# A two-layer graph network on one NeuronCore: edge keys before the normalisation, the adjacency zeroed by GpSimd, its totals made by DMA, relations fetched two ahead

## The reference

```python
def rgcn(x):                                  # in block 1
    out = x @ root + bias
    for r in range(8):
        mask = (edge_type == r)
        sums = segment_sum(x[src] * mask, dst)
        cnt = segment_sum(mask, dst)
        out = out + sums / max(cnt, 1) @ weight[r]
    return out
# block 1: a gated relational GNN
xn = layernorm(x); u = rgcn(xn)
z = concat([u, xn]) @ w_gate + b_gate
x = x + tanh(u) * z + xn * (1 - z)
# block 2: x = x + int8_linear(layernorm(x)), one scale for the whole input, from its largest magnitude
# block 3: x = x + D^-1/2 A D^-1/2 (layernorm(x) @ W.T + b), A the edges of all relations with self loops
# block 4: x = x + top-2 mixture of 8 experts + 0.1 * a shared expert, of layernorm(x)
```

## Time and profile before

| | us |
|---|---|
| median of 3 runs | 1464.07 (1456.95 to 1470.3) |
| the profiled execution | 1455.25 |
| its span | 1453.2 |
| PE busy, instructions | 1152.1 (79%), 5203 |
| DVE, POOL, ACT busy | 765.1, 432.5, 388.9 |
| mean granted TensorE clock | 0.888 |
| DMA | 200.76 MB, mean 138 GB/s |

### The profile page before, as it was taken

One profiled execution on the slowest core, in us unless ns is written; L12 is line 12 of the kernel. 1 busy time (PEld: TensorE's weight loads), 2 busy tenths in 40 slices (PEclk: granted clock), 3 DMA queues, 4 the chain that ended last, 5 costly groups with the idle time before them and its releaser, 6 DMA issues.

```text
span 1453.2 us, 13715 instructions
## 1 busy us (share of the span) xinstructions
PE 1152.1 (79%) x5203; PEld 906.0 (62%) x5203; DVE 765.1 (53%) x1230; ACT 388.9 (27%) x647; POOL 432.5 (30%) x284
## 2 busy tenths in 40 slices
PE   2659999999999999629466677756982899778993
PEld 1447777777777777517345455544861687657872
DVE  2429767867776412112345445443628747646644
ACT  1112232232223223011222222211414333315751
POOL 1005554445464555600111111110054501230023
PEclk8779999999999999859678888867995999979996
DMA  8554476765554444222322222234360210177855
GB/s 313 207 190 132 129 188 190 220 173 174 162 127 144 139 97 134 22 97 96 119 98 103 105 102 100 112 134 146 100 187 0 72 58 30 41 202 253 291 177 159
DMA packets 82465, 200.76 MB, mean 138 GB/s; under 512 B 33658, under 2 KB 34271, under 8 KB 73694
## 3 DMA queue, kind: packets, MB, share of 16 engines
q1 hardware_dynamic: 27444, 131.49, 26.1%
q0 software_dynamic: 35040, 21.99, 9.5%
q10 hardware_dynamic: 19908, 46.30, 9.0%
HBM read 141.21 MB, written 58.52 MB: 137 GB/s over the span
## 4 chain that ended last, share of the span: by engine, by line
PE 36%; DMA 31%; DVE 14%; POOL 8%; issue 5%; ACT 2%; ACTq 2%; SPq 1%; POOLq 0%; DVEq 0%
PE ps L481 30%; DMA stage<-h_scratch 8%; DMA adj_scratch<-cnt,idx 5%; POOL adj_scratch L1754 5%; DVE rl L334 5%; DMA AT<-adj_scratch 4%; DMA acb<-adj_scratch 3%; DMA stage<-in_w_e 3%; DMA stage<-in_w_gate 2%; DMA X<-in_x 2%; ACTq L948 1%; DVE U L1301 1%; DMA xn_scratch<-U 1%; ACT rh L326 1%; PE ps L743 1%
## 5 line engine op out<-in xcount | busy, mean ns | idle before, releaser
L334 DVE TENSOR_TENSOR rl<-stage,rh 128x512 fp32r<-128x512 f32 (+1 forms) x330 | 255.6, 805 | 488.4 <-ACT rh L326 488.3
L481 PE MATMUL ps<-rh,xTh 128*125 128x512 f32 x880 | 353.9, 402 | 75.3 <-DVE He L1273 39.6
L326 ACT CAST rh<-stage 128x512 fp32r<-128x512 f32 (+1 forms) x344 | 203.1, 622 | 646.6 <-PE ps L481 241.8
L481 PE MATMUL ps<-rl,xTh 128*125 128x512 f32 x880 | 351.7, 400 | 0.0
L481 PE MATMUL ps<-rh,xTl 128*125 128x512 f32 x880 | 349.8, 398 | 0.0
L1754 POOL DMA_INDIRECT adj_scratch<-cnt,idx x164 | 266.9, 1628 | 276.7 <-DMA adj_scratch<-cnt,idx 122.9
L481 PE MATMUL ps<-rh,Ar 125*125 125x512 f32 x400 | 173.9, 435 | 110.7 <-DVE rc L1291 96.0
L481 PEld LDWEIGHTS ps<-rh,xTh 128*125 128x125 f32 x880 | 165.9, 188 | 119.9 <-DVE He L1273 40.0
L481 PEld LDWEIGHTS ps<-rh,xTl 128*125 128x125 f32 x880 | 165.8, 188 | 43.0
L481 PEld LDWEIGHTS ps<-rl,xTh 128*125 128x125 f32 x880 | 165.8, 188 | 40.5
L481 PE MATMUL ps<-rl,Ar 125*125 125x512 f32 x400 | 170.0, 425 | 2.3 <-issue 2.3
(11 more groups left out here) (265 smaller groups left out, 1260.2 us busy)
## 6 DMA issues: line engine op xcount, KB each, us to landing
stage<-in_w_rel SPq DMA_DIRECT2D x32, 1024.0 KB
h_scratch<-He ACTq DMA_DIRECT2D x80, 250.0 KB
stage<-in_w_e SPq DMA_DIRECT2D x16, 1024.0 KB
adj_scratch<-Z ACTq DMA_DIRECT2D x16, 763.5 KB, 13.3
stage<-h_scratch SPq DMA_DIRECT2D x16, 750.0 KB
KR<-key_scratch ACTq DMA_DIRECT2D x41, 256.0 KB, 5.3
stage<-in_w_gate SPq DMA_DIRECT2D x8, 1024.0 KB
stage<-h_scratch SPq DMA_DIRECT2D x16, 500.0 KB
```

Of the source, the lines that this page charges most:

```text
L326: e.copy(h, s).then_inc(*a_hi.up(("hi", i)))
L334: e.tensor_tensor(l, s, h.bitcast(F32), ALU.subtract).then_inc(*own.up(("lo", i)))
L481: ins = e.matmul(ps[0:P, b, :], a, m, start=first and n == 0, stop=last and n == len(parts) - 1)
```

## The change

The edge keys come first: ACT issues the edge loads, DVE makes the keys before it normalises the first chunk, and PE turns them before anything else. The windows have TG = 5 tiles, so that there are 33 of them in place of 41, two to a half of a unit, and the first is made ahead of the second half of unit 0; the keys fill 83 rows in place of 82. The sixteen zeroing DMAs are issued by POOL once all of x is in. The normalised input is no longer stored: `x` is loaded again during relation 1, and ACT makes `XL` (the normalised input) and `X` (x plus it) from that and the statistics kept in `keep`. He has 6 slots. In stage 2 SP loads adjacency 0 and 1 after the first half of h(0), and then relation r + 2 after h(r). The counts come from `Sr`, the sum of the five chunks of `Ar` that DVE makes (`sources_summed`), times a column of ones. The total is made by eight DMAs of POOL from `adj_scratch`, the last seven accumulating. `Atot` lies where `AT` is to be, and is turned in place, five blocks at a time, after each chunk of block 2; DVE's degree sum and inverse roots move into and behind the gate. DVE adds into U before it makes the low parts, not after.

The sizes:

```diff
-TILES = 164
-TG = 4
+TILES = 165
+TG = 5
+KROWS = 83
-NHE = 8
+NHE = 6
-WINDOWS = (0, 2, 5)
+WINDOWS = (0, 4)
```

SP:

```diff
             def adjacency_in(r):
                 on.wait_ge(*at("added", TILES - 1))
+                on.wait_ge(*at("slot zero"))
                 if r >= 2:
                     on.wait_ge(*at("adj", r - 2))
...
-            adjacency_in(0)
             for r in range(R):
                 for g in range(first("h", r, 0, 0), first("h", r, 0, 0) + 4):
+                    if r == 0 and g == first("h", 0, 1, 0):
+                        adjacency_in(0)
+                        adjacency_in(1)
                     if g < first("gate", 0, 0) - 1:
                         load(g)
-                if r + 1 < R:
-                    adjacency_in(r + 1)
+                if r + 2 < R:
+                    adjacency_in(r + 2)
+                if r == 1:
+                    on.wait_ge(*at("unit", R + 1, 1, C - 1))
+                    e.dma_start(XL[:], x_v).then_inc(*d_xl.up(("x again",)))
...
-            on.wait_ge(*at("xn"))
-            e.dma_start(XL[:].rearrange("p c d -> p (c d)"), xnd).then_inc(*d_xl.up(("xl",)))
...
-            for c in range(C):
-                on.wait_ge(*at("spread", R - 1, 1, C - 1))
-                e.dma_start(X[:, c, :], x_v[:, c, :]).then_inc(*d_xc[c].up(("x again", c)))
```

PE, the counts of stage 2 (in place of ten column sums and five turns a relation), and the turns of the total behind each chunk of block 2:

```diff
+            def counts(r):
+
+                b, freed = banks.take(("counts", r), ("numbers", r))
+                on.wait_ge(*at("sources summed", r))
...
+                for c in range(C):
+                    ins = e.matmul(ps[0:P, b, 2 * c:2 * c + 2], Sr[:, r % 2, c * P:(c + 1) * P], ones2[:], start=True, stop=True)
...
+            for r in range(R):
+                if r:
+                    counts(r)
                 freed = lambda hf: lambda c: ("u", r + 1, c, hf)
+                by_tile(("spread", r, 0), tile["h", r, 0, 0], C, a_stat(r), freed(0), (("adj", r),), most_turned if r == R - 1 else None)
+                if r == 0:
+                    counts(0)
                 if r < R - 1:
                     by_tile(("spread", r, 1), tile["h", r, 1, 0], C, a_stat(r), freed(1), (("adj", r),))
...
+                for n, (i, j) in enumerate(swaps(c)):
+                    ins = e.transpose(ps[0:P, pair[n // 4][0], n % 4 * P:n % 4 * P + P], part_of(Atot, i, j), ident[0:P, 0:P])
```

ACT (of each `def` and loop the lines that matter):

```diff
+            for i, a in enumerate((src, dst, typ)):
+                on.wait_ge(*at("er zero", i))
+                e.dma_start(er[i][:, 0, :], a[0:EDGES0].rearrange("(p q) -> p q", q=128)).then_inc(*d_edge.up())
...
+            on.wait_ge(*at("key rows"))
+            e.dma_start(keyd.rearrange("(g p) q -> p g q", g=2), kr1[:]).then_inc(*d_key.up(("keys out",)))
             root("n1", 0)
             turned("n1", 0, xTh, ("pad",))
             highs(4)
-            for place in adj_zeros:
-                on.wait_ge(*at("Z"))
-                e.dma_start(place, Z[:]).then_inc(*d_zero.up(("adj zero",)))
+            for g in range(4):
+                key_rows(g)
...
-                        if r == 0 and hf == 0 and k == 0:
-                            adjacency_copy(1)
-                if 2 <= r + 2 < R:
-                    adjacency_copy(r + 2)
...
+                    if hf == 0 and r + 1 < R:
+                        adjacency_copy(r + 1)
+                if 2 <= r <= 6:
+                    c = r - 2
...
+                    e.activation(XL[:, c, :], XL[:, c, :], ACT.Identity, bias=keep[0][:, c:c + 1], scale=sm[:, 3, c:c + 1]).then_inc(*a_row.up(("xn", c)))
...
+            for c in range(C):
+                on.wait_ge(*at("spread", R - 1, 1, C - 1))
+                on.wait_ge(*at("xn", c))
+                e.activation(X[:, c, :], XL[:, c, :], ACT.Identity, bias=mv[:, c, 0:1], scale=keep[1][:, c:c + 1]).then_inc(*a_row.up(("x plus xn", c)))
...
+                for n, (i, j) in enumerate(swaps(c)):
+                    e.copy(part_of(AT, j, i), ps[0:P, banks.of["adj turn", c, n // 4], n % 4 * P:n % 4 * P + P]).then_inc(*a_out.up(("at", c)))
```

DVE:

```diff
+            def sources_summed(r):
...
+                for c in range(1, C):
+                    if c > 1:
+                        on.wait_ge(*at("sources summed", r))
+                    e.tensor_tensor(Sr[:, r % 2, :], a[:, 0, :] if c == 1 else Sr[:, r % 2, :].bitcast(F32), a[:, c, :], ALU.add).then_inc(
+                        *v_row.up(("sources summed", r)))
...
-                    for k in range(C):
-                        lows(tile["h", r, hf, k] + RT)
...
                     for c in range(C):
                         on.wait_ge(*at("spread", r, hf, c))
...
+                    for k in range(C):
+                        lows(tile["h", r, hf, k] + RT)
+                    if hf == 0 and r + 1 < R:
+                        sources_summed(r + 1)
+                    if hf == 1:
+                        mean_scales(r + 1)
...
             lows(tile["gate", 1, 0] + RT)
+            on.wait_ge(*at("self loops"))
+            e.tensor_reduce(deg[:, 0, :], Atot[:], AX, ALU.add).then_inc(*v_row.up(("degree",)))
...
+            inverse_degrees()
             on.wait_ge(*at("row max", C - 1))
```

POOL:

```diff
-            for c in range(C):
-                on.wait_ge(*at("n1", "norm", c))
-            e.dma_start(xnd, U[:].rearrange("p c d -> p (c d)")).then_inc(*d_xn.up(("xn",)))
+            for c in range(C):
+                on.wait_ge(*at("x", c))
+            for place in adj_zeros:
+                on.wait_ge(*at("Z"))
+                e.dma_start(place, Z[:]).then_inc(*d_zero.up(("adj zero",)))
...
-                    e.tensor_tensor(flat, flat, arf, ALU.add).then_inc(*p_row.up(("total", r)))
...
             for r in range(R):
-                total(r)
+                on.wait_ge(*(at("total", r - 1) if r else at("added", TILES - 1)))
+                e.dma_start(Atot[:], adjacency(r), accum_op=ALU.add if r else ALU.bypass).then_inc(*d_tot.up(("total", r)))
...
-            for c in range(C):
-                on.wait_ge(*at("x again", c))
-                on.wait_ge(*at("xn"))
-                e.dma_start(X[:, c, :], xnd[:, c * D:(c + 1) * D], accum_op=ALU.add).then_inc(*d_xs[c].up(("x plus xn", c)))
```

More of the change, by code:

```diff
@@ L584, in tensor, with most_turned @@
+            def most_turned(k):
+                if k == 3:
+                    b, freed = banks.take(("most",), ("most",))
                     on.wait_ge(*at("most of each"))
@@ L655, in tensor @@
             end_chunks(("gnn", 1))
-            took = [banks.take(("rest", c)) for c in range(C)]
+            took = [banks.take(("rest", c)) for c in range(C + 2)]
             on.wait_ge(*at("flag"))
@@ new lines, in mean_scales @@
+            def mean_scales(r):
+                on.wait_ge(*at("counts", r))
+                numbers = ps[0:P, banks.of["counts", r], 0:2 * C].rearrange("p (c a) -> p c a", a=2)[:, :, 0]
+                e.tensor_scalar(cn[:, r, :], numbers, 1.0, None, ALU.max).then_inc(*v_out.up(("numbers", r)))
+                on.wait_ge(*at("numbers", r))
+                e.reciprocal(rc[:, r, :], cn[:, r, :]).then_inc(*v_row.up(("rc", r)))
+            e.scalar_tensor_tensor(out=keep[0], in0=mv[:, :, 0], scalar=-1.0, in1=sm[:, 3, :], op0=ALU.mult, op1=ALU.mult).then_inc(*v_row.up())
```

376 lines of the change are left out of this document (151 added, 225 removed).

## The result

The changed kernel takes 1504.39 us (median of 4 runs, 1492.88 to 1514.32) against 1465.74 for the kernel before on the same chip: ratio 1.0268, interval 1.0175 to 1.0362. It is slower by 39 us, where 80 us less were forecast; that is clear of no change, though the lower end of the interval lies under two per cent. The profiled execution is 1508.7 us, its span 1506.9 against 1453.2.

A forecast was written before the change was run, and what follows sets the result against it. Stage 1 was taken as PE-bound, stage 2 as DMA-bound at 127 GB/s. Start 38, hand-over 41, stage 2 and tail -18, behind the gate 21, block 2 -2: 80 us off 1464 gives 1384; range 1312 to 1445.

The forecast's parts named there:

- All three idles can go: Start: PE's idles of 18.70, 9.06 and 13.54 us before its long run of products vanish; 3.5 us added.
- the 41 us of the hand-over: Stage 1 to stage 2: 41 us lost before the change, all to be won by the earlier scatter and new order.
- 9.4 of each engine if spread over all: Stage 2: one total costs 150 engine-us, 9.4 us of each engine; six of eight totals add 56 us.
- Rival 4: Stage 2: totals use the loads' five engines, 30 us each, six times: +124, 1508 us; chance 0.09.
- 1384 again: Rival 4's variant: each total takes five consecutive engines from a moving cursor, 30 us each; the whole stays 1384 us.
- the five engines: All 125-partition loads, mainly in stage 2, share five DMA engines, bounding them at 127 GB/s together.
- rival 2: Stage 2: the order isn't better, holes stay 8 us a relation, 64 in place of 16: 1432 us; chance 0.18.
- ring: Stage 2: closed chain of waits, 39 us a relation, seen in the profile after; not in the prediction.
- DVE follows PE: Behind the gate: POOL ends before DVE is through gate half 0, so the int8 scale comes 66 us after G'.
- 1: Rival 1, stage 2: totals are cheap or overlap, stage 2 is 304, 72 less: 1312 us; chance 0.14.
- 3: Rival 3: stage 2 becomes PE-bound, 8 x 23.3 us from B': 1227 us; chance 0.03.
- 5: Rival 5: the scatter is late, at 17 us a group ending 67 us later: about 1445 us; chance 0.06.

The follow-up runs named there:

- e4: Changed kernel with the nine edge loads issued by SP ahead of the loads of x, instead of by ACT: 1504.26 us.
- e8: e4 with the store of the key rows as two transfers, rows 0 to 79 and rows 80 to 82: 1482.89 us.
- e9: Kernel before with adjacency 0 loaded behind the first half of h(0), nothing else changed: 1461.37 us, ratio 0.994 to the kernel before.
- e14: Changed kernel with adjacency 0 ahead of relation 0's first h loads again, adjacency 1 still behind them: 1509.74 us.
- e1: Changed kernel with the first total transfer alone, the seven adding ones left out (incomplete, for timing only): 1421.80 us.
- e2: Changed kernel with all eight total transfers as plain copies that don't add (incomplete, for timing only): 1467.23 us.
- e13: Changed kernel with each total as two transfers, rows 0 to 119 and 120 to 124, loads unchanged: 1480.39 us.
- e5: e1 with ACT's copy of the next adjacency and DVE's sums of it moved ahead of the tiles of the relation's first half: 1401.84 us.

## Why the prediction was wrong

The forecast's span was 1373, the measured one 1506.9; the 134 us between them by the prediction's own steps (A' is the start of the long run of products, B' the first spread product, G' the first gate product, Q' the int8 scale):

| step | predicted | measured | difference |
|---|---|---|---|
| start, A' | 64 | 99.7 | +36 |
| A' to B' | 531 | 534.9 | +4 |
| B' to G' (stage 2 and the way to the gate) | 372 | 449.0 | +77 |
| G' to Q' | 66 | 75.9 | +10 |
| Q' to the end | 340 | 347.4 | +7 |

*Start: the step failed.* "All three idles can go", with 3.5 us for the edge loads, was the step. They went, and a wait of 46.6 us came in their place: PE's turn of the keys, now its first instruction, stood until 46.60. I costed nine small loads and a store by their bytes. ACT alone stood 34 us in the issue of three of these loads (chain after, line 940). What counts is that they run beside the loads of x: e4 moves the wait from the loads to the store, and e8 takes it off the chain by rows 0 to 79. The store of the key rows on few engines was in the prediction, at 4 us of bytes, and the 42.24 us of e4 are ten times that. The prediction has it on one engine by the rule of the Trainium skill, and e8 agrees with the rule. I had written that the keys' DMAs ahead of ACT's roots and casts are the wait that could return; it did return, and had no size.

*Scatter, stage 1, hand-over: right.* 33 groups in 478 us, 14.5 each for 14.2. Of the 41 us of the hand-over 37 were won. I put the gain down to the order and the earlier scatter together; e9 and e14 bear both out, and neither says how much is whose. That adjacency 0 would land at about B' held in the changed kernel (631.6) and was in part luck: in e1, e2 and e13 it landed 8 to 22 us later, and PE idled for it.

*Stage 2: the step that turned the sign.* Two parts. First the totals: 56 us forecast, 92 measured (e1). The size of one total was right, 96 engine-us a MB: 37.5% of 16 engines for 20 us and 1.25 MB is 96 again. What failed is "9.4 of each engine if spread over all": the earlier trace rows showed a chunk of X over sixteen, and the total went to about five at a time, 40.3 us to land, so six or seven of them lay across the loads for 265 us. The 92 us over these are some 14 each, where 9.4 was taken. Rival 4 had the kind, at 0.09, but not the price: its 30 us each would be 180. That its 1508 lies near the measured 1504 is luck, for its sum has a start 36 us too early and a stage 2 that is 47 us too long (372 + 124 for 449). Its "1384 again", if the five engines moved on from transfer to transfer, failed too: the share of 0.69 against 0.25 agrees with engines that move, and the loads lost all the same.

Second, the order: without totals I had 316 us, and e1 has 356.6, 40 more. This is rival 2, put at 48 us and 0.18. Its ring is one that I didn't see. I let the four sums "lie in the 9 us a half in which these engines wait for DMA", but they wait for the copy of the adjacency, which on ACT stands behind the casts of the h tiles that come with it, and PE has the counts ahead of the spread. Loads two relations ahead don't help an operation that is queued behind the last load. e5 takes the ring out: 21 us in stage 2, and the load engines hold the rest. Nor had I the wait of adjacency 1 for the last writes of zx, 28.12 us in the chain of e1; in the kernel before SP's load of adjacency 1 stood 9.64 us for the same writes.

*The five engines: right*, and the largest thing in the kernel. I used them to bound a sum and didn't ask what it takes to leave them.

*Behind the gate: the size was off.* 75.9 for 66: "DVE follows PE" failed, since eight low parts at 1.55 us beside POOL and a degree sum of 3.32 on DVE made DVE the last. *Block 2 and later*: +9 for +2 against before. Up to the gh products, behind block 2, it is about 3 (they start 95.7 us behind the scale, for 92.8); the experts take 6 us more, whose cause was not looked for.

*Rivals.* 1 fell with e1 and e2; 3 with stage 2 at 449 us; 5 came to nothing (574.8, 24 us before SP asks); its own numbers, 17 us a group, give 1451 and not 1445. That two rivals would both come true, and the start fail as well, was in no case of mine: with chances put on one at a time, their sum had no place.

## What to carry to other kernels

Count the engines of a transfer before its bytes: the number of rows decides, and the same loads as 120 and 5 rows instead of 125 took 77 us off the kernel with one total, while each of seven adding transfers of 125 rows beside them cost it 12 us. A small transfer that something waits for can't be priced by its bytes when large ones run beside it: 83 KB took 42 us. And a prefetch gains only what its consumer's place in each in-order queue lets through: follow the first use of the data, not its landing.

## What the runs showed that was not expected

An adding DMA from DRAM to SBUF of 1.56 MB landed in 40.3 us and a plain one in 28.9 beside the same loads; spread over fifteen engines the adding one's 120 rows took 12.7. It took 96 engine-us a MB, the plain loads 40. The store of 83 KB in 83 rows took 42.24 us beside x. Beside POOL's add of 6.34 us one DVE operation on SBUF took 6.22 us in place of 0.82, and the same add in five pieces of 1.86 us (median) stretched the sums to 1.8 (median) and 2.04 at most.
